# Moving the weight splits of a graph network's layers from GpSimd to ScalarE and VectorE

## What is computed

```
x = _layernorm(x + _L0_gnn_ref(x, Ws_self, Ws_neigh, bs, src, dst))
x = _layernorm(x + _L1_gnn_ref(x, mesh_nfeat, edge_index, edge_attr_4, ...))

def _L0_gnn_ref(x, Ws_self, Ws_neigh, bs, src, dst):
    for l in range(3):
        neigh = segment_sum(h[src], dst) * inv_deg
        h = h @ Ws_self[l] + neigh @ Ws_neigh[l] + bs[l]
        if l != 2:
            h = relu(h)
```

## Time and profile before

| | |
|---|---|
| median of 3 runs | 2476.69 us (2476.14 to 2477.04) |
| the profiled execution, its own time | 2471.52 us |
| its span in the trace | 2469.8 us |
| PE busy in the span | 2264.8 us, 92% |
| DVE, ACT, POOL busy | 58%, 47%, 46% |
| phase B, first to last instruction | about 425 to 784 us |

### The profile page before, as it was taken

The page is one execution under the profiler, slowest core; times in us unless marked ns, Lnnn a source line. Parts: engine busy times, 40 slices in busy tenths (PEclk is TensorE's granted clock), DMA queues, the critical chain, the costliest instruction groups (busy, mean ns, idle before and its releaser), DMA issues. The chain is left out here.

```text
span 2469.8 us, 44190 instructions
## 1 busy us (share of the span) xinstructions
PE 2264.8 (92%) x13410; PEld 1918.9 (78%) x13413; DVE 1424.1 (58%) x3084; ACT 1169.6 (47%) x2117; POOL 1148.0 (46%) x1677
## 2 busy tenths in 40 slices
PE   2988487899987799999999999999999999999897
PEld 1436487777765688888888888888888888888776
DVE  7012298534562566666666666666666666666566
ACT  0121011323211666666666666666666666666431
POOL 4777601001200455555555555555555555555333
PEclk9999799899998899999999999999999999999999
DMA  6223100001023533333323323233333333233121
GB/s 190 76 53 80 19 0 0 35 5 35 24 89 97 152 61 61 63 63 59 59 59 64 64 60 59 59 64 60 62 62 59 61 62 62 61 59 60 30 93 43
DMA packets 76280, 149.70 MB, mean 61 GB/s; under 512 B 14689, under 2 KB 15789, under 8 KB 76219
## 3 DMA queue, kind: packets, MB, share of 16 engines
q0 software_dynamic: 44864, 93.18, 19.8%
q1 hardware_dynamic: 31243, 55.63, 6.8%
q10 hardware_dynamic: 112, 0.11, 0.0%
HBM read 129.12 MB, written 19.46 MB: 60 GB/s over the span
## 5 line engine op out<-in xcount | busy, mean ns | idle before, releaser
L1260 DVE CUSTOM_DVE_ANT_0 c_var_bank<-c_var_bank,c_p,k_floor 128x512 f32<-128x512 f32 x176 | 133.5, 759 | 369.9 <-PE c_var_bank L1417 369.9
L1151 POOL DMA_INDIRECT c_from_src<-s_dst_table,c_at_nodes x176 | 284.0, 1614 | 32.0 <-issue 32.0
L1471 PE MATMUL c_edge_bank<-c_m_hi,c_pt_hi 128*128 128x512 f32 x704 | 292.1, 415 | 0.0
L1145 POOL DMA_INDIRECT c_from_src<-s_mesh_table,c_at_nodes x176 | 206.5, 1173 | 152.2 <-POOL c_at_nodes L1141 142.9
L1472 PE MATMUL c_edge_bank<-c_m_lo,c_pt_hi 128*128 128x512 f32 x704 | 276.9, 393 | 0.0
L1473 PE MATMUL c_edge_bank<-c_m_hi,c_pt_lo 128*128 128x512 f32 x704 | 275.5, 391 | 0.0
L1157 POOL TENSOR_TENSOR c_dev<-c_var,k_half 128x1 f32<-128x1 f32 x176 | 97.9, 556 | 381.2 <-DVE c_var L1247 381.2
L319 POOL DMA_INDIRECT s_records<-a_stage_rec,a_stage_row x170 | 205.2, 1207 | 56.8 <-issue 48.8
L1415 PE MATMUL c_var_bank<-c_m_hi,c_pt_hi 128*128 128x384 f32 x704 | 226.9, 322 | 4.5 <-ACT c_var_bank L1340 4.5
L1366 ACT ACTIVATE c_h<-c_from_src 128x512 f32<-128x512 f32 x176 | 111.2, 632 | 248.8 <-DVE c_from_src L1279 248.8
L1415 PE MATMUL c_var_bank<-c_m_hi,c_ht_hi 128*128 128x384 f32 x704 | 226.5, 322 | 0.1
(11 more groups left out here) (311 smaller groups left out, 6058.2 us busy)
## 6 DMA issues: line engine op xcount, KB each, us to landing
k_w<-in_L_gnn_Ws_self_dram SPq DMA_DIRECT2D x3, 1024.0 KB, 9.9
k_w<-in_L_gnn_Ws_neigh_dram SPq DMA_DIRECT2D x3, 1024.0 KB, 13.0
c_from_src<-s_mesh_table,c_at_nodes POOLq DMA_INDIRECT x176, 3.5
c_from_src<-s_dst_table,c_at_nodes POOLq DMA_INDIRECT x176, 4.7
s_records<-a_stage_rec,a_stage_row POOLq DMA_INDIRECT x170, 2.6
a_mesh<-in_L_gnn_mesh_nfeat_dram SPq DMA_DIRECT2D x10, 250.0 KB
k_h<-in_x_dram SPq DMA_DIRECT2D x1, 2500.0 KB
s_mesh_table<-a_mesh_out SPq DMA_DIRECT2D x10, 250.0 KB
```

Source lines behind the costliest of these rows:

```text
L1145: pool.indirect_dma_start(from_src[u][:], None, scratch["mesh_table"], bass.IndirectOffsetOnAxis(ap=at_nodes[u][:, 0:1], axis=0)).then_inc ...
L1151: pool.indirect_dma_start(from_src[u][:], None, scratch["dst_table"], bass.IndirectOffsetOnAxis(ap=at_nodes[u][:, 1:2], axis=0), compute_o ...
L1260: dve.tensor_tensor_reduce(var1_bank[:], var1_bank[:], p[u % 2][:], 1.0 / D, k["floor"][:, 0:1], ALU.mult, ALU.add, var[u][:, 0:1]).then_i ...
L1471: pe.matmul(edge_bank[:], left[0], m_hi[1][:, c, :], start=False, stop=False, skip_group_check=True)
```

## The change

POOL's splits go. The second layer's split is made in phase A: after its last product block ACT waits for the load of the matrices and makes both high parts, and DVE the low parts, before it waits for the edge records. The two later splits stand in the neighbour sums of q = 1 and q = 2: ACT makes a high part after blocks 1 and 3, DVE the low part after blocks 2 and 4. The semaphore `w_split` now counts single matrices. SP no longer waits before its first load of matrices in phase B (layer three's), and before its second it waits for the two low parts of q = 1. SP's wait for `w_next` in phase A is now ACT's.

```diff
@@ phase_a, sync @@
-        sp.wait_ge(w_next, 32)
         sp.wait_ge(bias_next, 16)
@@ phase_a, vector @@
                               ALU.subtract).then_inc(u_lo_ok, 1)
+        for i in range(2):
+            dve.wait_ge(w_next_hi, i + 1)
+            dve.tensor_tensor(w_lo[i][:], w[i][:], w_hi[i][:].bitcast(F32), ALU.subtract).then_inc(w_next_lo, 1)
         dve.wait_ge(recs_in, 16)
@@ phase_a, scalar @@
             act.activation(u_hi[:, n, :], neigh_bank[n % 2][0:NPB, :], ACT.Copy).then_inc(u_hi_ok, 1)
+        act.wait_ge(w_next, 32)
+        for i in range(2):
+            act.activation(w_hi[i][:], w[i][:], ACT.Copy).then_inc(w_next_hi, 1)
@@ phase_b, sync @@
         for r in range(1, LAYERS):
-            sp.wait_ge(w_split, r)
+            if r > 1:
+                sp.wait_ge(w_split, 2 * r - 2)
             for i in range(2):
                 sp.dma_start(w[i][:], chunked(products[r][i])).then_inc(w_in, 16)
@@ phase_b, gpsimd @@
-        for r in range(LAYERS):
-            if r:
-                pool.wait_ge(w_in, 32 * r)
-                pool.wait_ge(prod_mm, NB * r)
-            for i in range(2):
-                pool.tensor_copy(w_hi[i][:], w[i][:]).then_inc(split_step, 1)
-            pool.wait_ge(split_step, 2 * r + 2)
-            pool.tensor_tensor(w_lo[0][:], w[0][:], w_hi[0][:].bitcast(F32), ALU.subtract)
-            pool.tensor_tensor(w_lo[1][:], w[1][:], w_hi[1][:].bitcast(F32), ALU.subtract).then_inc(w_split, 1)
@@ phase_b, vector @@
+        def split(r, j):
+            dve.wait_ge(w_hi_ok, 2 * r - 1 + j)
+            dve.tensor_tensor(w_lo[j][:], w[j][:], w_hi[j][:].bitcast(F32), ALU.subtract).then_inc(w_split, 1)
...
                 mix(q, i)
+                if q and i in (2, 4):
+                    split(q, i // 2 - 1)
                 if q == LAST and i % 2:
                     normalise(i - 1)
@@ phase_b, scalar @@
                     act.activation(h[:, node(i), :], mixed[i % 2][:], ACT.Relu).then_inc(h_ok, 1)
+                if q and i in (1, 3):
+                    act.wait_ge(w_in, 32 * q)
+                    act.wait_ge(prod_mm, NB * q)
+                    j = i // 2
+                    act.activation(w_hi[j][:], w[j][:], ACT.Copy).then_inc(w_hi_ok, 1)
@@ phase_b, tensor @@
             if i == 0:
-                pe.wait_ge(w_split, r + 1)
+                need(pe, w_split, 2 * r)
```

More of the change, by code:

```diff
@@ L206, in phase_a @@
     prod_mm, self_ok, u_hi_ok, u_lo_ok = (sem(n) for n in ("prod_mm", "self_ok", "u_hi_ok", "u_lo_ok"))
-    w_next, bias_next = sem("w_next"), sem("bias_next")
+    w_next, bias_next, w_next_hi, w_next_lo = (sem(n) for n in ("w_next", "bias_next", "w_next_hi", "w_next_lo"))
     def spread(b):
@@ L730, in phase_b @@
     many_ok, many_mm, many_read = sem("many_ok"), sem("many_mm"), sem("many_read")
-    w_split, split_step = sem("w_split"), sem("split_step")
+    w_hi_ok, w_split = sem("w_hi_ok"), sem("w_split")
     hc_ok, turned, ht_hi_ok, ht_lo_ok, prod_mm = (
```

## The result

| | median | runs |
|---|---|---|
| before | 2476.41 us | 2475.06 to 2477.04, 4 runs |
| changed | 2526.07 us | 2520.88 to 2531.86, 4 runs |

The ratio is 1.0202, with a 95% interval of 1.0178 to 1.0226. So it is slower clear of noise, by about 2%. The forecast was 2464.0 us. The profiled execution of the changed kernel took 2524.34 us, its span 2522.6.

A forecast was written before the change was run, and what follows sets the result against it. PE bounds most neighbour sums, POOL's scatter phase A, DVE phase B's start and the last layer's sums. Terms +2.7 - 12.0 + 0.6 - 4.0 = -12.7 us gave a 2464.0 us median, range 2459.0 to 2470.0 us.

The forecast's parts named there:

- The change part by part: Sum of four local terms, phase A, start of phase B, q = 1 and q = 2: -12.7 us.
- the one on the slower side: Neighbour sums of q = 1 and q = 2: PE falls to 1.2 GHz, 2491 us; chance 4%.
- The four terms together: Phase A, start of phase B, q = 1 and q = 2: +2.7 - 12.0 + 0.6 - 4.0 = -12.7 us.
- Phase A: +2.7 us: Phase A: DVE's two subtractions lengthen two of POOL's scatter transfers; their own cost is covered; +2.7 us.
- Start of phase B: -12.0 us: Phase B's start: without POOL's split, four slow DVE instructions fall to undisturbed times; -12.0 us.
- rival 3: Phase B's start: no speedup, as instructions are new after the barrier or another engine is late; 2476.0 us; chance 6%.
- q = 1: +0.6 us: Neighbour sums of q = 1: ACT's high parts make PE wait about 1.1 us once, 0.5 us gained; +0.6 us.
- q = 2: -4.0 us: Last layer's sums: first `x` additions undisturbed, low parts fall into DVE's waits for `x`; -4.0 us.
- the difference of the profiled execution from the median: Whole kernel: profiled 2471.52 us lies 5.17 us under the 2476.69 us median; same difference taken off both kernels.

The follow-up runs named there:

- a_notick5: Changed kernel without DVE's ten `tick` semaphore increments (nothing waits on them) in the last layer's normalisation, five executions: 2458.82 us, ratio 0.9928.
- b_dve6: Kernel before with six semaphore increments that nothing waits for added on DVE in a last-layer product block: 2536.65 us, ratio 1.0243.
- a_dve64: Changed kernel with 64 more idle semaphore increments on DVE in a last-layer product block: 2459.64 us, ratio 0.9931.
- b_act10: Kernel before with ten idle semaphore increments added on ACT in a last-layer product block: 2476.97 us, ratio 0.9998.
- b_dve3: Kernel before with three idle semaphore increments added on DVE in a last-layer product block: 2472.85 us profiled, one execution.
- a_spread: Changed kernel without the ten increments, second high part on ACT after block 4, second low part on DVE after block 5: 2458.07 us, ratio 0.9923.
- a_first: Changed kernel without the ten increments, the two later splits back on POOL, only the second layer's split moved: 2460.65 us, ratio 0.9934.

## Why the prediction was wrong

**The step that failed** is the sum itself, in "The change part by part". It costs six subtractions more on DVE and four copies on ACT where they run, and calls them free where they are covered. It had no term for what instructions added to an engine's program do to the code behind them. The edge loop of phase C appears in no term: nothing in it is edited. That missing term measured +66.1 us in the profiles (1745.6 against 1679.5) and +67.3 us by medians (2526.07 against 2458.82 of a_notick5, which leaves out ten increments of the changed kernel). Run b_dve6 shows that it needs none of the rest of the change, and a_dve64 that it comes from the place and not from the number. What the forecast lacked is a load of code behind each of 19 jumps back, 66.1 / 19 = 3.5 us each. Of the rivals, the one on the slower side (PE at 1.2 GHz in the sums) named another mechanism, and it did not occur: the granted clock was 1.00 over 541 to 640 us, which holds all sums of q = 1, and in q = 2 it fell once for some microseconds (0.79 over 652 to 660), as it had before the change (0.79 over 684 to 692). That the forecast had 62% and all slower cases 4% was an error of the same kind, since all rivals were drawn from the stages that the change edits.

**The four terms together** were right: -12.7 us. One pair of profiles gives -13.34 at phase C's start, but kernels that are the same up to there differ by 2.3 us. Four profiles with the splits of the kernel before (before, b_act10, b_dve3, b_dve6) have this start at 789.24 to 791.58 us, 790.4 in the mean. Seven with those of the change (all but a_spread and a_first) have it at 776.98 to 778.14, 777.7 in the mean. That is 12.7 us.

**Phase A: +2.7 us** was right in kind and near in size. The lengthened transfers are 2.45 and 1.89 us, 1.27 + 0.71 = 1.98 us over the usual 1.18, and the first one-hot tile comes 1.94 us later (303.50 against the earlier trace rows). The other runs with the changed phase A have 2.06 to 3.30 and 1.88 to 1.91 us, 1.6 to 2.8 us in all, except for a_spread, in which the subtractions met two of POOL's small copies instead (1.76 and 2.35 us, where they take 0.20 and 0.29 in a_notick5). The one-hot tile comes at 304.2 us in the mean of these nine profiles and at 301.6 in the mean of the four others. DVE's low parts ran from 275.85 to 280.34 us, 2 us later than I had worked out, and still 23.16 us ahead of that tile, so this cost nothing. The Trainium skill has a probe in which such a subtraction didn't stall GpSimd's transfers ("SBUF — State Buffer", section "Who interferes with whom"). That is not borne out here, by two transfers of the trace before and two of this one. Another 0.61 us appeared between the one-hot tile and phase B (427.52 against the earlier trace rows), for which I had no term; this stretch took 123.4 us in the kernel before and 124.9 in b_dve6, which is the same up to there, so 0.6 us isn't to be told from chance.

**Start of phase B: -12.0 us** measured -11.9: PE's first sum came 14.99 us behind DVE's first instruction of the phase before, and 430.63 - 427.52 = 3.11 us after. Subtractions that took 2.55 and 5.07 us take 0.82 and 0.81 as soon as POOL is idle, so rival 3 (instructions new after the barrier) is out. PE still runs at 1.2 GHz after this idle, as expected: its first product takes 0.79 us, and the granted clock was 0.61 over 430 to 436 us and 1.00 over 436 to 440.

**q = 1: +0.6 us** measured +0.57, start to first product: 551.34 to 599.45 before, 541.55 to 590.23 after. PE waits once, 0.71 us, for a conversion, at the block that was named.

**q = 2: -4.0 us** measured -4.1 (the lead over before goes from 9.22 us at the start of q = 2 to 13.34 at the start of phase C). I had not expected how it comes: 3.1 us of it is in the sums, and the rest behind them. The additions of `x` take 1.28 us in each of the first three pairs, and both low parts fit into what had been DVE's wait for `x`. In the fourth and fifth pair, where no low part stands, DVE waits for `x` again (2.12 and 2.93 us), which I had thought gone.

**The median against the profile.** The prediction took the difference of the profiled execution from the median, 5.17 us, as a fixed one, and with the place of the loop mended its sum would have given 2464.0 us. The kernels without the loss measured 2458 to 2461 us. Most of this is not a gain of the change. Run b_act10 has the structure and, to 0.2 us, phase C's start (790.51) of the kernel before, and its span is 5.7 us longer. The timeline of PE where phase C ends, and one of PE's last products (start, duration), of b_act10:

```profile
2334.34 0.79 PE L1445 MATMUL c_sum_p_bank<-c_rp_hi,c_hot 128*128 128x512 f32 x1 [3.26 <-DVE c_hot L1228]
...
2344.12 0.79 PE L1445 MATMUL c_sum_p_bank<-c_rp_hi,c_hot 128*128 128x512 f32 x1 [4.30 <-DVE c_hot L1228]
...
2465.19 0.63 PE L1780 MATMUL d_node_bank<-d_m_hi,d_nt_lo 128*125 128x512 f32 x1
```

and of the kernel before:

```profile
2334.02 0.49 PE L1442 MATMUL c_sum_p_bank<-c_rp_hi,c_hot 128*128 128x512 f32 x1 [3.26 <-DVE c_hot L1225]
...
2341.21 0.79 PE L1442 MATMUL c_sum_p_bank<-c_rp_hi,c_hot 128*128 128x512 f32 x1 [4.15 <-DVE c_hot L1225]
...
2459.67 0.40 PE L1777 MATMUL d_node_bank<-d_m_hi,d_nt_lo 128*125 128x512 f32 x1
```

After the same idle of 3.26 us PE runs at 1.2 GHz in one (0.79; granted clock 0.66 over 2330 to 2340 us) and at 2.4 GHz in the other (0.49; 0.97), and the next sums come 9.78 us later instead of 7.19: 2.6 us. At the last products it is so again (0.63 and 0.40): b_act10 lies 3.3 us behind until the last 20 products, and 5.5 at the last one. In the profiled execution of before both fell well; its median is 5 us longer. So what I took as a constant was most likely this scatter. Of the 18.1 us between the medians (2476.93 and 2458.82) some 13 are the change's, read at phase C's start. The rest may be a difference in how often these two places fall well. In a_notick5's profile the first did (0.49 after 3.62 us of idle), and the mean granted clock of its executions is 0.972 to 0.974, against 0.969 to 0.972 before. But a_dve64 is as fast with 0.971, so this is not shown, and why the kernel with 13 us less should gain 5 us more stays open.

## What to carry to other kernels

Before a change adds or takes instructions on an engine, look for long loops behind them in its program: here a loop of 302 instructions on DVE at a place six further on cost 66 us, five times what the change had gained, and ten instructions less gave the gain back. The count alone didn't say which places are slow. What told was to run the kernel with a few idle instructions more or less ahead of the loop. In the profile this looks like nothing that was edited: a longer idle time behind each jump back to a loop's start, put down to "issue" or to an operation that happened to end just before, and more packets on the queue for instructions (122 for 27), so compare that row of two kernels first when a change loses time in a stage that it doesn't touch. A local gain is read at a checkpoint, the first instruction of the next phase, and not from the total: the forecast was right there to 0.7 us in one pair of profiles and to 0.1 in the mean of several, while the total was wrong by 62.

## What the runs showed of the hardware that was not expected

- Three added instructions decide. Between three and six semaphore increments on DVE lies a step from 2472.85 to 2537.12 us. As no run lay between the two levels, it is probably a single one.
- The cost of the same loading, 122 packets, was 66, 32, 64 us at the places +6, +22 and +38: 3.5, 1.7 and 3.4 us behind each of the 19 jumps back.
- Each jump back brings five packets of 8.2 KB. Why five isn't explained by any run.
- ACT's loop, moved by ten places (b_act10), kept its 27 packets and its time. ACT's loop is shorter, and whether it has a slow stretch of its own wasn't tried.
- DVE's subtraction of 125x1280 int16 took 2.55 and 5.07 us beside POOL's large instructions, and 0.82 and 0.81 with POOL idle. In phase A it is DVE's 4.49 us of float32 subtraction that lengthens POOL's indirect transfers, 1.18 to 2.45 and 1.89 us. The hindrance goes both ways.
